# Smaller target groups, compact query denominators and VectorE's weight remainders in a graph-transformer layer

## The reference, cut to what matters

```python
xn = layernorm(x)
# graph convolution: deg counts edges per target, dinv = deg ** -0.5
out = segment_sum((xn @ W)[src] * (dinv[src] * dinv[dst])[:, None], dst); gnn = relu(out + b)
# linear attention, 16 heads of 64
phiQ, phiK = elu(xn @ Wq + bq) + 1, elu(xn @ Wk + bk) + 1
S = phiK.T @ V;  Z = phiK.sum(0)
context = (phiQ @ S) / (phiQ @ Z + 1e-6)
x = x + gnn + context @ Wo + bo
# feed-forward
h = silu(ln @ w1 * s1) * (ln @ w2 * s2); h = gelu(h @ h1 * s3); h = gelu(h @ h2 * s4)
x = x + h @ w3 * s5          # ln = layernorm(x)
```

## Time and profile before

| what | before |
|---|---|
| median of 3 runs | 995.62 us |
| profiled execution, its time | 995.84 us |
| its span | 994.1 us |
| TensorE busy | 975.2 us, 98% |
| TensorE weight loads busy | 824.4 us, 83% |
| VectorE busy | 543.9 us, 55% |
| ScalarE busy | 293.6 us, 30% |
| GpSimd busy | 142.4 us, 14% |
| L1212, 24 reciprocals | 65.9 us |
| L1076 and L1077, one-hots | 41.8 and 42.1 us |

### The profile page before, as it was taken

How to read it: one execution, slowest core, us unless ns; L and a number is a source line. 1 busy time by engine, 2 the same in 40 slices (tenths; PEclk the granted TensorE clock), 3 DMA queues, 4 the chain that set the end, 5 groups by cost and what they waited for, 6 DMA issues and landing times.

```text
span 994.1 us, 13325 instructions
## 1 busy us (share of the span) xinstructions
PE 975.2 (98%) x4860; PEld 824.4 (83%) x4860; DVE 543.9 (55%) x1067; ACT 293.6 (30%) x585; POOL 142.4 (14%) x191
## 2 busy tenths in 40 slices
PE   5999999999999999999999999999999999999998
PEld 4887888888889989978786788767788999999986
DVE  6886578777763888782113556447557212122354
ACT  6873122232133343341213221114113312135300
POOL 7101001001011050050300000000201103064100
PEclk9999999999999999999999999999999999999999
DMA  7412013113021022122201465535422302010053
GB/s 269 150 49 86 5 30 117 28 31 100 16 77 36 26 90 73 52 69 95 96 12 55 147 204 172 157 119 186 170 80 90 123 1 85 1 43 1 22 190 139
DMA packets 46979, 86.78 MB, mean 87 GB/s; under 512 B 19036, under 2 KB 23388, under 8 KB 46896
## 3 DMA queue, kind: packets, MB, share of 16 engines
q1 hardware_dynamic: 38416, 57.28, 17.5%
q0 software_dynamic: 8480, 28.45, 8.7%
HBM read 61.62 MB, written 24.09 MB: 86 GB/s over the span
## 4 chain that ended last, share of the span: by engine, by line
PE 92%; DVE 3%; DMA 2%; ACT 1%; issue 1%; POOL 1%; SPq 0%; DVEq 0%; ACTq 0%; POOLq 0%
PE PS L1431 11%; PE PS L1433 11%; PE PS L1432 11%; PE PS L1552 9%; PE PS L1553 9%; PE PS L1554 9%; PE PS L1610 5%; PE PS L1612 4%; PE PS L1630 3%; PE PS L1631 3%; PE PS L1629 3%; PE PS L1471 2%; PE PS L1446 2%; PE PS L1683 2%; PE PS L1682 2%; PE PS L1681 2%
## 5 line engine op out<-in xcount | busy, mean ns | idle before, releaser
L1431 PE MATMUL PS<-ring,act_t 128*128 128x512 f32 (+1 forms) x480 | 194.7, 406 | 1.3 <-POOL ring L443 0.6
L1433 PE MATMUL PS<-ring,act_t 128*128 128x512 f32 (+1 forms) x480 | 190.7, 397 | 0.0
L1432 PE MATMUL PS<-ring,act_t 128*128 128x512 f32 (+1 forms) x480 | 190.3, 396 | 0.0
L1552 PE MATMUL PS<-act_t,ring 128*128 128x416 f32 (+1 forms) x432 | 159.3, 369 | 1.4 <-POOL ring L443 1.3
L1553 PE MATMUL PS<-act_t,ring 128*128 128x416 f32 (+1 forms) x432 | 152.2, 352 | 0.0
L1554 PE MATMUL PS<-act_t,ring 128*128 128x416 f32 (+1 forms) x432 | 151.7, 351 | 0.0
L1431 PEld LDWEIGHTS PS<-ring,act_t 128*128 128x128 f32 (+1 forms) x480 | 89.8, 187 | 23.9 <-POOL ring L443 1.6
L1433 PEld LDWEIGHTS PS<-ring,act_t 128*128 128x128 f32 (+1 forms) x480 | 89.5, 186 | 22.4
L1432 PEld LDWEIGHTS PS<-ring,act_t 128*128 128x128 f32 (+1 forms) x480 | 89.9, 187 | 21.2 <-issue 0.5
L1552 PEld LDWEIGHTS PS<-act_t,ring 128*128 128x128 f32 x432 | 81.3, 188 | 6.8 <-issue 3.4
L1553 PEld LDWEIGHTS PS<-act_t,ring 128*128 128x128 f32 x432 | 81.4, 188 | 4.0 <-issue 3.4
(11 more groups left out here) (195 smaller groups left out, 1650.7 us busy)
## 6 DMA issues: line engine op xcount, KB each, us to landing
stage_x<-in_wslices_dram POOLq DMA_DIRECT2D x54, 256.0 KB, 4.2
stage<-in_wslices_dram POOLq DMA_DIRECT2D x42, 256.0 KB, 3.7
xr<-x_d SPq DMA_DIRECT2D x18, 512.0 KB, 3.6
phin_d<-phiq SPq DMA_DIRECT2D x8, 625.0 KB, 3.1
xrow<-in_x_dram SPq DMA_DIRECT2D x9, 512.0 KB, 3.6
xh<-in_x_dram SPq DMA_DIRECT2D x18, 256.0 KB
x_d<-xh SPq DMA_DIRECT2D x18, 256.0 KB
x_d<-xr SPq DMA_DIRECT2D x9, 512.0 KB, 3.0
```

What stands on the lines that cost most here:

```text
L1431: pe.matmul(out_ap, node_rows(0, k, t), ring[:, slot(k0 + k), 0, :], start=(k == 0), stop=False)
L1432: pe.matmul(out_ap, node_rows(1, k, t), ring[:, slot(k0 + k), 0, :], start=False, stop=False)
L1433: ins = pe.matmul(out_ap, node_rows(0, k, t), ring[:, slot(k0 + k), 1, :], start=False, stop=(k == KD - 1))
L1552: pe.matmul(out_ap, w[0], x_t[:, 0, k, o:o + n], start=(k == 0), stop=False)
```

## The change

1. **Groups of 10 targets.** `WIN` goes from 13 to 10, `STATIC_CHUNKS` from 4 to 3 (384 keys). A tile has 13 groups (the last of 8 targets), the last tile 10: 127 in all. Two neighbouring groups make a part, which shares one pair of one-hot instructions and one copy of counts; 59 parts have two groups, nine have one. Three parts go in each of the steps 12 to 34. No group of this input has more than 384 edges (the largest has 381). SyncE reads up to seven bounds with one register load.
2. **Compact denominators.** The order of query units is f fastest within a slab of four: unit i is f = 4s + r % 4, c = r // 4 with s, r = divmod(i, 12). Four units of one c (a group g) add into one PSUM tile of 8 rows, two heads for each. phiQ and the key sums are split in an fp32r copy (ScalarE, L858 and L874) and a remainder (VectorE, L1277), and three fp32r matmuls with 8 weight columns replace the fp32 one. One reciprocal of 8 rows serves four units; it is stored to DRAM and spread from there over 64 rows a head, in four parts (`rec_spread`). The product follows eight units behind, and phiQ is stored by unit instead of by block.
3. **Remainders.** VectorE makes the weight remainders of slices 42 to 57, eight behind the sum of iteration 10 and eight behind that of iteration 22; GpSimd only reloads the staging buffers there.

```diff
-STATIC_CHUNKS = 4
+STATIC_CHUNKS = 3
-OH_BUFS = 5
+OH_BUFS = 4
-WIN = 13
+LOADED = 7
+WIN = 10
-PHI_BUFS = 3
+PHI_BUFS = 9
+PHI_LAG = 8
...
+PARTS = [(t, j, min(2, groups_of(t) - j)) for t in range(NT) for j in range(0, groups_of(t), 2)]
...
-    if 12 <= step < 37:
-        return list(range(4 * (step - 12), 4 * (step - 11)))
+    if 12 <= step < 35:
+        return list(range(3 * (step - 12), min(3 * (step - 11), len(PARTS))))
...
+            def rec_spread(g, j):
+                n = CHUNKS[g % 3][1]
+                sp.wait_ge(rec_stored, 16 * (g + 1))
+                if g >= 1:
+                    sp.wait_ge(phin_ready, 4 * (g - 1) + j + 1)
+                for h in range(2):
+                    sp.dma_start(rec_all[64 * h:64 * h + 64, j, 0:n],
+                                 rec_d[g, j, h:h + 1, 0:n].to_broadcast([64, n])).then_inc(rec_in[j], 16)
...
-                for j in range(WPT):
+                for j in range(0, groups_of(dt), LOADED):
...
+                    _, firsts = nc.values_load_multi_w_load_instructions(bounds[0:1, w:w + m], engines=[mybir.EngineType.SP],
+                                                                         min_val=0, max_val=LAST_FIRST)
...
-            def slab_rest(first):
-
-                for n in range(first, first + 6):
-                    weight_lo(nc.gpsimd, n)
...
-            slab_rest(42)
-            slab_rest(50)
+            for n in range(42, 58):
+                reload(n)
...
+            def phi_split(i):
+                n = CHUNKS[q_chunk(i)[1]][1]
+                act.wait_ge(phiq_ready, i + 1)
                 if i >= 2:
...
+                    act.wait_ge(phi_used, i - 1)
+                nc.scalar.activation(phi_hl[:, 0, i % 2, 0:n], phiq[:, i % PHI_BUFS, 0:n], ACT.Copy).then_inc(phi_hi, 1)
...
-                if i >= 2:
-                    den_copy(i - 2)
...
+                if i >= 1:
+                    phi_split(i - 1)
+                if i >= 5 and i % 4 == 1:
+                    den_copy((i - 5) // 4)
...
             for i in range(24):
                 q_min(i)
-                if i >= 3:
-                    den_invert(i - 3)
+                if i == 1:
+                    z_rest()
+                if i >= 1:
+                    phi_rest(i - 1)
+                if i >= 6 and i % 4 == 2:
+                    den_invert((i - 6) // 4)
+                if i >= PHI_LAG:
+                    den_apply(i - PHI_LAG)
                 q_add(i)
-                if i >= 3:
-                    den_apply(i - 3)
+                if i % 12 == 10:
+                    for n in range(42 + 8 * (i // 12), 50 + 8 * (i // 12)):
+                        weight_lo(dve, n)
...
-                pe.matmul(PS[:, 3 + i % 2, 0:n], zblk[:, f, :], phiq[:, f % PHI_BUFS, o:o + n],
-                          start=True, stop=True).then_inc(den_done, 1)
+                pe.wait_ge(phi_lo, i + 1)
+                if j == 0 and g >= 2:
+                    pe.wait_ge(den_read, g - 1)
+                for z, b in ((0, 0), (0, 1), (1, 0)):
+                    ins = pe.matmul(PS[0:8, 3 + g % 2, 0:n], z_hl[:, z, i // 12, 8 * j:8 * j + 8], phi_hl[:, b, i % 2, 0:n],
+                                    start=(j == 0 and z + b == 0), stop=(j == 3 and z == 1))
+                ins.then_inc(phi_used, 1)
```

More of the change, by code:

```diff
@@ L108, in rows, with q_chunk @@
     return min(P, N - t * P)
+def q_chunk(i):
+    s, r = divmod(i, 12)
+    return 4 * s + r % 4, r // 4
 def units():
     u = [("kv", s, t) for s in range(4) for t in range(NT)]
-    u += [("q", 0, 0), ("z", 0), ("z", 1)]
-    u += [("q", f, c) for f in range(KD) for c in range(3) if f or c]
+    u += [("q", 0, 0), ("z", 0)]
+    u += [("q", *q_chunk(i)) for i in range(1, 24)]
     u += [("h", 0, t) for t in range(NT)]
@@ L151, in sums_of, with width, parts_through @@
     return step + 1 + (step + 1) // NT
-def width(w):
-    return min(WIN, P - w % WPT * WIN)
+def width(j, m=1):
+    return min(WIN * m, P - j * WIN)
+def parts_through(t):
+    return sum(p[0] <= t for p in PARTS)
 def tile_ended(step):
-    return [w // WPT for w in windows_of(step) if w % WPT == WPT - 1]
+    return [PARTS[w][0] for w in windows_of(step) if w + 1 == parts_through(PARTS[w][0])]
 def build(nc, x, src_rows, dst_rows, wslices, wo, bkv, bq, gb, bo, scales, w3s, out):
@@ L321, in build @@
         phiq_ready = sem("phiq_ready")
-        den_done = sem("den_done")
+        z_hi = sem("z_hi")
+        phi_hi = sem("phi_hi")
+        phi_lo = sem("phi_lo")
+        phi_used = sem("phi_used")
+        rec_stored = sem("rec_stored")
+        rec_in = [sem(f"rec_in{j}") for j in range(4)]
         den_read = sem("den_read")
@@ L498, in _ @@
                         keys_load(dt + KEY_BUFS)
-                if step >= 40 and (step - 40) % 3 == 2 and (step - 40) // 3 >= 1:
-                    phin_store((step - 40) // 3 - 1)
-            phin_store(KD - 1)
+            for i in range(24 + PHI_LAG):
+                g, late = divmod(i - 6, 4)
+                if late == 0 and 0 <= g < 6:
+                    rec_store(g)
+                if i >= PHI_LAG:
+                    phin_store(i - PHI_LAG)
+                if late == 0 and 0 <= g < 6:
+                    for j in range(3):
+                        rec_spread(g, j)
+                if late == 1 and 0 <= g < 6:
+                    rec_spread(g, 3)
             for b in range(PHI_BUFS):
-                sp.wait_ge(phin_stored[b], 16 * len(range(b, KD, PHI_BUFS)))
+                sp.wait_ge(phin_stored[b], 16 * len(range(b, 24, PHI_BUFS)))
             for b in range(2):
@@ L684, in _ @@
             for b in range(PHI_BUFS):
[L685 removed]
+                pool.wait_ge(phin_stored[b], 16 * len(range(b, 24, PHI_BUFS)))
             for b in range(2):
@@ L828, in _ @@
                 if i % 12 == 11:
-                    for k in range(42 + 8 * (i // 12), 48 + 8 * (i // 12)):
+                    for k in range(42 + 8 * (i // 12), 50 + 8 * (i // 12)):
                         hi(k)
@@ L1534, in key_sums @@
                 pe.wait_ge(ksum_ready, 40)
-                for i in range(2):
-                    u = UNIT["z", i]
-                    b = open_unit(u)
-                    for j in range(4):
-                        ins = pe.matmul(PS[:, b, P * j:P * (j + 1)], ksum[:, P * (4 * i + j):P * (4 * i + j + 1)], ones[:],
-                                        start=True, stop=True)
-                    ins.then_inc(acc_full, 1)
+                u = UNIT["z", 0]
+                b = open_unit(u)
+                for f in range(KD):
+                    ins = pe.matmul(PS[:, b, f:f + 1], ksum[:, P * f:P * (f + 1)], ones[:, 0:1], start=True, stop=True)
+                ins.then_inc(acc_full, 1)
             def gemm_cols(u, f, c, k0, nk, x_t, first, last):
```

226 lines of the change are left out of this document (123 added, 103 removed).

## The result

The changed kernel takes 1010.83 us (median of five runs, 1009.04 to 1012.67), the kernel before 996.12 us beside it (995.32 to 998.2). The ratio is 1.0143, its 95% interval 1.0131 to 1.0154. The forecast was 991.6 us, its range ended at 1000. So it shows 13.2 of the 14.7 us.

What follows compares the result with a forecast made beforehand. The prediction took the kernel as TensorE-bound (busy 98%); its terms, -6.6 - 3.1 - 0.4 + 5.3 + 4.2 - 3.4 = -4.0 us from 995.84, gave 991.8, and 991.6 us for the median, range 985 to 1000.

Steps and rivals of the forecast that it cites:

- 13 loads for 10: Key/value stage: SyncE issues 13 loads a tile instead of 10; priced at 0, bound +1 us.
- last sign of being wrong: Key/value stage: the prediction is wrong if TensorE waits for a count part there; no size given.
- Rival 1: GpSimd's code switch comes late, behind the count loads; slices 58 to 63 are 4.6 us late: 996.2 us; chance 0.28.
- Rival 2: Clock falls while TensorE stands 3.7 us before denominators 10 and 22, 7.4 us in all: 999 us; chance 0.10.
- the stalls: Slab changes: TensorE waits for VectorE before denominators 10 and 22, +5.3 and +4.2 us, bounds 0 and +8 each.
- Rival 3: No stall at the slab changes, VectorE's order looser or reciprocal on 8 rows short: 982 to 986 us; chance 0.12.
- What goes with GpSimd's remainders: Slab changes: taking the weight remainders off GpSimd saves 3.4 us over both, bounds 0 and -3.6.
- Counts: Key/value stage: 381 narrower count matmuls in 23 steps instead of 25 steps of 1.06 us: -6.6 us, bounds -1.3 and -8.2.
- Denominators: Query units: three fp32r products at 0.57 us replace the fp32 one at 0.70: -3.1 us, bounds -4.3 and +3.
- Key sums: Eight fp32 products with one column instead of 128: -0.4 us, bounds 0 and -1.7.
- The round trip of the reciprocals: Query stage: store to DRAM and eight spreads have 7 us, covered by 1.5 us; uncovered, up to 6 x 2 us.
- The row that the prediction took as proof that 1.66 us do no harm: Trace near the start: a wait of 1.66 us did not bring TensorE's low clock back.

Runs made afterwards that it cites:

- filled waits: Changed kernel plus 14 unread TensorE matmuls before each of denominators 10 and 22: 1008.24 us.
- the last kernel: Changed kernel with three key tiles ahead, early GpSimd switch, interleaved VectorE remainders, slab changes begun earlier, product 3 before the fp32r remainder: 982.7 us.

## Why the prediction was wrong

**The waits' end at SyncE was looked for at one place only (5.5 us).** The prediction counted 13 loads for 10, asked when the first tile's keys come, and gave 0 with a bound of +1. It did not name what is queued behind: behind the 52 loads stands the store of tile 0, behind that ScalarE's copy, behind that TensorE. Its last sign of being wrong, TensorE waiting for a count part in the key/value stage, is what came. Two runs move the wait in both directions: the time changed by -5.8 us with 13 loads fewer ahead of the store and by +6.6 us with slower loads.

**Rival 1 was the mechanism, not the exception (8.0 us).** The late switch was described place by place and given 0.28, at 4.6 us. It happened, and the pause was 9.54 us, not 6.16, with the low clock behind TensorE's wait. The argument against it, that code in use from the start needs no loading, fell: the Trainium skill (GPSIMD Engine Reference, 2.1 Instruction dispatch) gives about 6 us for the first call to a freshly loaded kernel, the traces agree with 6.1 to 6.6 for the all-reduce, and the way back costs 6.6 to 9.9 as well. That loading code fills the pause is inferred; the runs show that the pause goes with the first ordinary instruction behind the all-reduce.

**Rival 2 too, at a smaller price (6.4 us, over four waits).** Given 0.10. The low clock followed each of the four waits of 3.4 to 4.2 us, for 3.4 us, and took 1.6 us a time, not the 3.7 that were read from the start. The filled waits show it for two of them; for the other two it is read from the pace alone. Where the low clock lasted 6.8 us, in other executions, it took more, 0.9 us more at the first slab change of the run with three tiles of keys ahead. The range missed because three things that the prediction priced one at a time came together: they are separate places, and their chances were not exclusive.

**The slab changes: the stalls are right (5.3 and 4.2 predicted), the clock behind them was not in them.** TensorE stood 3.55 and 3.43 us before denominators 10 and 22, with slices late before it; the losses without the clock, 5.4 and 4.3 us, are those of the run with filled waits. Rival 3 is out. What goes with GpSimd's remainders was put at -3.4. By the count used here the kernel before loses 2.2 and 1.6 us at the slab changes, the last kernel 0.1 and 0.0. With the reciprocal at the same place, GpSimd's remainders cost 4.9 us more than VectorE's interleaved ones (991.74 against 986.81), in part by the low clock.

**The savings.** Counts: -6.6 predicted; -5.8 up to unit 0, with the wait gone. The prediction's prices give a gap of 0.37 + 18 x 0.045 + 0.1 = 1.28 us, where 1.34 was measured; over 23 steps that is 1.4 us. Its own subtraction, 26.5 - 19.5, gives 7.0 and not 6.8. Denominators: -0.13 us a unit predicted, -0.15 measured; the upper bound of +3 doesn't follow from 0.25 us each, which gives 24 x 0.05 = 1.2. Key sums: -0.4 predicted and 0 measured; passes of one column are 0.11 us apart, as those of 128 were. The round trip of the reciprocals is covered as worked out: VectorE never waited for a spread.

So the sum of the prediction's own terms held in the main: -4.0 us predicted, some -3.5 by these figures (-5.8, 24 x -0.15, 0, and 5.4 + 4.3 - 2.2 - 1.6 at the slab changes). The steps that failed are outside it: the wait behind SyncE's loads, put at 0, the wait behind GpSimd's pause and the low clock, left to rivals, made some 17 us on top (5.5, 8.0 and twice 1.6).

## What to carry to other kernels

When a change adds instructions to a queue, follow that queue to its next store or wait, not only to the data that the new instructions bring: here the twelve loads more cost nothing by themselves and 5.5 us through the store behind them. A block of work moved to an engine with half its time free still stops the kernel if it sits between two links of a chain; the same instructions spread over three iterations, with one product moved ahead, cost 0.1 us. Mechanisms at different places add up: price them as a sum with chances, not as rivals of which one comes true. When an experiment takes one wait away, compare the place as well as the total: the low clock comes and goes with the other waits and moved a total by up to 4 us here.

## What the hardware showed

- GpSimd pays on the way back as well: 6.64 to 7.62 us (four runs) between its all-reduce and the next ordinary instruction when that stands right behind, 9.27 to 9.91 us (five runs) when it stands behind count loads much later.
- In the profiles of before, after and eleven experiments all 18 waits of TensorE between 3.4 and 7.6 us had the pace of 1.2 GHz behind them. Of 17 waits between 1.3 and 1.8 us four had it and thirteen had not, at the same place of the same instructions (near 22 us) in three executions out of thirteen. The row that the prediction took as proof that 1.66 us do no harm was one draw. And one long wait isn't needed: with GpSimd's remainders the low clock came behind three and four waits of 0.33 to 0.75 us in a row, in two executions, and in the run with one bound to a load behind two of 1.19.
- Fp32r matmuls with 8 weight columns run as fast as those with 128: 0.19 us apart at 416 columns, their weight load included. The key sums' fp32 passes with one column are as far apart as with 128: 0.11 us.
- A reciprocal on 8 rows takes 2.73 us, one on 128 rows 2.74: the time doesn't depend on the rows, and compact denominators save VectorE time only by being inverted four at a time.
- Beside GpSimd's remainders VectorE's two-input instructions take up to 1.66 us where they take 0.59 elsewhere, more than the 1.31 that was read from before. A GpSimd remainder that started together with a reciprocal on 8 rows took 4.26 and 4.27 us where others take 1.3 to 1.45: about what was left of the reciprocal, 2.7, and one remainder.
